# Attention scores made by two halves of TensorE's array instead of the whole one, in a gated cross-attention and mixture-of-experts layer

## What is computed

```python
qh = (q @ Wq + bq).reshape(B, LQ, 16, 32).transpose(0, 2, 1, 3)      # q = layernorm(x)
kh = (k @ Wk + bk).reshape(B, 128, 16, 32).transpose(0, 2, 1, 3)     # k = v = ctx_512
vh = (v @ Wv + bv).reshape(B, 128, 16, 32).transpose(0, 2, 1, 3)
attn = softmax(einsum('bhqd,bhkd->bhqk', qh, kh) / sqrt(32))
x = x + tanh(g_xattn[0]) * (concat(einsum('bhqk,bhkd->bhqd', attn, vh)) @ Wo + bo)
...
logits = clip(layernorm2(x) @ router_w.T); top_v, top_i = top_k(logits, 2)
# each expert takes its tokens in order, up to a capacity of 1280
h = silu(xb @ w_gate.T) * (xb @ w_up.T); yb = h @ w3.T
x = x + tanh(g_ffn[0]) * (sum of the two experts' rows, weighted)
```

## Time and profile before

| | us |
|---|---|
| median of 3 runs | 2701.61 (2700.34 to 2702.97) |
| the profiled execution | 2701.12 |
| its span, first to last instruction | 2698.4 |
| TensorE busy | 2606.9 (97% of the span) |
| VectorE busy | 1395.5 (52%) |
| ScalarE busy | 948.5 (35%) |
| GpSimd busy | 419.9 (16%) |

### The profile page before, as it was taken

One profiled execution on the slowest core, in us unless ns is written; L12 is line 12 of the kernel. 1 busy time (PEld: TensorE's weight loads), 2 busy tenths in 40 slices (PEclk: granted clock), 3 DMA queues, 4 the chain that ended last, 5 costly groups with the idle time before them and its releaser, 6 DMA issues.

```text
span 2698.4 us, 40582 instructions
## 1 busy us (share of the span) xinstructions
PE 2606.9 (97%) x14168; PEld 2319.0 (86%) x14169; DVE 1395.5 (52%) x2644; ACT 948.5 (35%) x2481; POOL 419.9 (16%) x399
## 2 busy tenths in 40 slices
PE   7999999499999999999999999999999999999988
PEld 6887887499999888888888888888888999989987
DVE  5898888444444444444444444443444444445555
ACT  6766666222224222242222322332223322233343
POOL 5555555300002000020000300010001100030030
PEclk9999999699999999999999999999999999999999
DMA  9422222411113210132101511231012311132142
GB/s 343 162 93 80 100 90 73 163 65 46 47 47 58 87 47 23 47 62 86 47 23 47 114 60 47 77 84 47 23 47 64 82 47 47 47 79 111 70 127 81
DMA packets 58993, 208.37 MB, mean 77 GB/s; under 512 B 8516, under 2 KB 8796, under 8 KB 50562
## 3 DMA queue, kind: packets, MB, share of 16 engines
q1 hardware_dynamic: 42242, 175.30, 18.1%
q0 software_dynamic: 16640, 31.69, 6.1%
HBM read 145.60 MB, written 67.70 MB: 79 GB/s over the span
## 4 chain that ended last, share of the span: by engine, by line
PE 77%; issue 2%; DVE 1%; ACT 1%; DMA 0%; DVEq 0%; ACTq 0%; POOL 0%; POOLq 0%
PE bank L1580 76%; PE bank L1586 1%; DVE yacc L1520 0%; ACT slotsT_hi L1412 0%; DVE slotsT_lo L1489 0%; DVE h L1540 0%; DMA xrow<-expert_rows 0%; ACT yout L1436 0%; ACT later_hi L1408 0%; ACT h_hi L1450 0%; POOL out_dram L1394 0%; DVE w_lo L1483 0%; ACT silu L1444 0%; DVE early_lo L1483 0%; ACTq L1292 0%
## 5 line engine op out<-in xcount | busy, mean ns | idle before, releaser
L1540 DVE TENSOR_TENSOR h<-silu,bank 128x384 f32<-128x384 f32 (+2 forms) x320 | 183.8, 575 | 829.3 <-PE bank L1580 819.5
L1580 PE MATMUL bank<-slotsT_hi,early_hi 128*128 128x384 f32 (+2 forms) x1280 | 445.1, 348 | 13.3 <-issue 11.5
L1580 PE MATMUL bank<-slotsT_hi,w_hi 128*128 128x384 f32 (+2 forms) x1280 | 442.6, 346 | 5.9 <-DVE w_lo L1483 5.9
L1580 PE MATMUL bank<-slotsT_lo,early_hi 128*128 128x384 f32 (+2 forms) x1280 | 443.2, 346 | 1.7 <-issue 1.7
L1580 PE MATMUL bank<-slotsT_hi,early_lo 128*128 128x384 f32 (+2 forms) x1280 | 442.4, 346 | 0.0
L1580 PE MATMUL bank<-slotsT_lo,w_hi 128*128 128x384 f32 (+2 forms) x1280 | 442.1, 345 | 0.0
L1580 PE MATMUL bank<-slotsT_hi,w_lo 128*128 128x384 f32 (+2 forms) x1280 | 441.2, 345 | 0.0
L1450 ACT CAST h_hi<-h 128x384 fp32r<-128x384 f32 (+2 forms) x320 | 169.3, 529 | 746.2 <-DVE h L1540 746.2
L1444 ACT ACTIVATE silu<-bank 128x384 f32<-128x384 f32 (+2 forms) x320 | 162.5, 508 | 729.2 <-PE bank L1580 728.7
L1394 POOL DMA_INDIRECT out_dram<-yout,token x63 | 97.9, 1554 | 1976.5 <-ACT yout L1436 1675.7
L1520 DVE TENSOR_TENSOR yacc<-bank,yacc 128x512 f32<-128x512 f32 x464 | 316.8, 689 | 168.8 <-PE bank L1580 168.7
(11 more groups left out here) (199 smaller groups left out, 3549.4 us busy)
## 6 DMA issues: line engine op xcount, KB each, us to landing
staged<-in_moe_w_dram SPq DMA_DIRECT2D x33, 1536.0 KB, 6.4
raw<-in_moe_w_dram SPq DMA_DIRECT2D x32, 1536.0 KB, 6.4
xrow<-expert_rows SPq DMA_DIRECT2D x42, 520.0 KB, 8.2
expert_rows<-zeros SPq DMA_DIRECT2D x40, 520.0 KB, 8.6
xin<-in_x_dram SPq DMA_DIRECT2D x17, 512.0 KB, 3.7
xres<-in_x_dram SPq DMA_DIRECT2D x15, 512.0 KB, 3.7
out_dram<-xres SPq DMA_DIRECT2D x15, 512.0 KB, 3.1
staged<-in_L_xattn_Wq_dram SPq DMA_DIRECT2D x1, 1024.0 KB, 7.3
```

Source lines behind the costliest of these rows:

```text
L1540: nc.vector.tensor_tensor(h32[q % 2][:, 0:W], silu[q % 2][:, 0:W], UB[q % 2][:, 0:W], ALU.mult)\
L1580: last = nc.tensor.matmul(out_ap, st, mv, start=(at == 0), stop=(at == n - 1))
```

## The change

TensorE's array is used as two halves of 64 rows. Rows 0 to 63 hold heads 0 and 1 of a group, rows 64 to 127 hold heads 2 and 3, and each half makes its two heads' scores with 256 moving columns, so that the zero blocks that lay between the two pairs of heads are no longer streamed. Half c writes PSUM bank c. One call `scores(n, g)` makes both token tiles of a group: 12 matmuls of 256 columns, the halves taking turns, in place of two calls of three matmuls of 512 columns. A bank now holds two heads of both tiles instead of four heads of one tile, and `maxima` and `exps` go by bank, with the same number of instructions and elements as before. The call waits until the exps of the whole group before are done. Both banks are signalled at the end of the stretch.

In VectorE's order three of the eight `maxima` of a block move up: the fourth, the sixth and the eighth stand right behind the one before them.

```diff
+            HP = HG // 2
...
                     def exps(blk, idx):
 
-                        g, t = divmod(idx, 2)
+                        g, c = divmod(idx, 2)
                         act.wait_ge(max_ready, 2 * KD * blk + idx + 1)
                         if not isinstance(blk, int) or blk > 0:
-                            act.wait_ge(pt_ready, 2 * KD * (blk - 1) + idx + 1)
-                        for hh in range(HG):
-                            h = HG * g + hh
-                            ins = nc.scalar.activation(probs[:, t, h, :], S_BANK[t][:, hh * LKV:(hh + 1) * LKV], ACT.Exp,
-                                                       bias=neg_max[:, t, h:h + 1], accum_out=sums[:, t, h:h + 1])
+                            act.wait_ge(pt_ready, 2 * KD * (blk - 1) + 2 * g + 2)
+                        for t in range(2):
+                            for hh in range(HP):
+                                h, at = HG * g + HP * c + hh, (HP * t + hh) * LKV
+                                ins = nc.scalar.activation(probs[:, t, h, :], S_BANK[c][:, at:at + LKV], ACT.Exp,
+                                                           bias=neg_max[:, t, h:h + 1], accum_out=sums[:, t, h:h + 1])
                         ins.then_inc(exp_done, 1)
...
                     def maxima(n, idx):
-                        g, t = divmod(idx, 2)
+                        g, c = divmod(idx, 2)
                         dve.wait_ge(s_ready, 2 * KD * n + idx + 1)
-                        nc.vector.tensor_reduce(neg_max[:, t, HG * g:HG * (g + 1)],
-                                                S_BANK[t][:, :].rearrange("p (h t) -> p h t", h=HG),
+                        nc.vector.tensor_reduce(neg_max[:, :, HG * g + HP * c:HG * g + HP * (c + 1)],
+                                                S_BANK[c][:, :].rearrange("p (t h k) -> p t h k", t=2, h=HP),
                                                 AX.X, ALU.max, negate=True).then_inc(max_ready, 1)
...
-                    def scores(n, idx, b):
-                        g, t = divmod(idx, 2)
+                    def scores(n, g, b):
 
                         pe.wait_ge(q_lo, KD * n + g + 1)
-                        if not isinstance(n, int) or 2 * KD * n + idx >= 2:
-                            pe.wait_ge(exp_done, 2 * KD * n + idx - 1)
-                        passes(S_BANK[t][:, :], [((qT_hi[:, g, t * P:(t + 1) * P], qT_lo[:, g, t * P:(t + 1) * P]),
-                                                  (k_hi[b][:, g, :], k_lo[b][:, g, :]))]).then_inc(s_ready, 1)
+                        if not isinstance(n, int) or KD * n + g >= 1:
+                            pe.wait_ge(exp_done, 2 * KD * n + 2 * g)
+                        for t in range(2):
+                            for i, (qs, ks) in enumerate(((qT_hi, k_hi), (qT_hi, k_lo), (qT_lo, k_hi))):
+                                for c in range(2):
+                                    rows, keys_of = slice(c * HP * DK, (c + 1) * HP * DK), slice(c * HP * LKV, (c + 1) * HP * LKV)
+                                    last = nc.tensor.matmul(S_BANK[c][:, t * HP * LKV:(t + 1) * HP * LKV],
+                                                            qs[rows, g, t * P:(t + 1) * P], ks[b][rows, g, keys_of],
+                                                            start=(i == 0), stop=(i == 2))
+                                    if t == 1 and i == 2:
+                                        last.then_inc(s_ready, 1)
```

More of the change, by code:

```diff
@@ L855, in step @@
                             maxima(n, 2)
+                            maxima(n, 3)
                             q_rest(n, 1)
@@ L860, in step @@
                             x_rest(n + 1)
-                        if has(n, 0):
-                            maxima(n, 3)
                         if isinstance(n, int) and n == 0:
@@ L871, in step @@
                             maxima(n, 4)
+                            maxima(n, 5)
                         if has(n, 2):
@@ L874, in step @@
                         if has(n, 0):
-                            maxima(n, 5)
                             recips(n, 1)
@@ L884, in step @@
                             maxima(n, 6)
+                            maxima(n, 7)
                         if has(n, 1):
@@ L889, in step @@
                             pT_second(n, 0)
-                            maxima(n, 7)
                         if has(n, -2):
@@ L1069, in step @@
                             scores(n, 0, b_s)
-                            scores(n, 1, b_s)
                             if has(n, -3):
@@ L1078, in step @@
                                 values_made(0)
-                            scores(n, 2, b_s)
+                            scores(n, 1, b_s)
                         if has(n, 1):
@@ L1089, in step @@
                             heads(n - 1, 0, b_v)
-                        if has(n, 0):
-                            scores(n, 3, b_s)
                         if has(n, -1):
@@ L1096, in step @@
                         if has(n, 0):
-                            scores(n, 4, b_s)
+                            scores(n, 2, b_s)
                         if has(n, -2):
@@ L1104, in step @@
                             turn_rows(n - 2)
-                        if has(n, 0):
-                            scores(n, 5, b_s)
                         if has(n, -1):
@@ L1117, in step @@
                             probs_T(n, 0)
-                            scores(n, 6, b_s)
+                            scores(n, 3, b_s)
                         if has(n, -1):
@@ L1122, in step @@
                             attention_out(n - 1, 0)
-                        if has(n, 0):
-                            scores(n, 7, b_s)
                         if has(n, -2):
```

## The result

| | before | changed |
|---|---|---|
| median of 4 runs | 2701.12 us (2700.34 to 2702.97) | 2729.01 us (2723.40 to 2731.17) |
| span of the profiled execution | 2698.4 | 2727.2 |
| mean granted TensorE clock | 0.983 | 0.980 |

The changed kernel is slower: the ratio is 1.0099, with a 95% interval of 1.0082 to 1.0117. The forecast was 2720 (2703 to 2738), +18 where +28 came.

A forecast was written before the change was run, and what follows sets the result against it. The prediction took a loop over VectorE and GpSimd, with TensorE closing it together, to bound the attention blocks. 13 blocks at 1.4 us more gave 18 us on 2701.1, hence 2720 us, range 2703 to 2738.

The forecast's parts named there:

- rival A: Attention blocks: VectorE's new order lengthens the loop over VectorE and GpSimd, 2710 to 2732 us; chance 0.60.
- Step 1: Score matmuls on TensorE: the two row halves run fully parallel, 0.72 us a group instead of 1.38.
- Step 2: Score stretches on TensorE: entering and leaving the 64-row array shape costs 0.40 us a stretch, or nothing.
- Step 3: Group 1's scores wait some 0.8 us for group 0's exps; maximum 2 comes 0.58 later, 0.31 remaining.
- Step 4: VectorE's order: maxima ahead of the statistics and `q_rest` cost 0.60 us each, not given back; `q_rest` 1.51 later.
- Step 5: TensorE's side of the loop: its saved time becomes idle time ahead of `attention_out`, which starts 1.51 us later.
- Sum: Blocks 2 to 14: 1.4 us more for each of 13 blocks, 18 us in all; nothing for other blocks.
- Rival B: Attention blocks: TensorE sets the time and gets faster, 2685 us, or 2659 without shape cost; chance 0.11.
- D: Score matmuls: the halves don't overlap, 1.84 us a group, 28 us more, 2748 us; chance 0.08.
- C: Delays absorbed: `place`'s count doesn't wait for GpSimd and three or four clock drops vanish, about 2703 us; chance 0.12.
- E: TensorE's clock drops in every block from longer idle time, 14 us more, 2734 us; chance 0.09.
- theory V: Experiments' theory: VectorE and GpSimd close the loop, two moved maxima cost 0.60 us each a block, late signals the rest.

The follow-up runs named there:

- experiment 9: Changed kernel with SyncE's store of a block's output rows issued some 5 us later, behind the load of rows: 2724.55 us, 1.0091 of the kernel before.
- experiment 5: Changed kernel without GpSimd's four indirect writes of routing rows a block: 2704.86 us, one run.
- experiment 2: Kernel before with only maximum 7 (the eighth) moved ahead of `q_rest` in VectorE's order: 2719.25 us, 1.0069 of the kernel before.
- experiment 3: Changed kernel with scores by full 128-row matmuls of 512 columns, tile by tile, instead of halves: 2714.85 us, 1.0048 of the kernel before.
- experiment 11: Kernel before with maximum 7 ahead of `q_rest` and the output store behind the load: 2721.28 us, 1.0073 of the kernel before.

## Why the prediction was right, and where it was off

**Direction and mechanism (rival A) held.** The loop over VectorE and GpSimd sets the block: VectorE's order undone gives back 1.2 us a block and 13.7 us in all, half of the 28. The size of the sum came out right in part by luck, as its bullet below says.

- *Step 1, halves parallel*: held. Pairs every 0.12 us.
- *Step 2, 0.40 for the change of shape*: close. The rows show 0.1 behind the first pair, 0.09 ahead of the query and 0.1 ahead of its follower, 1.0 us of TensorE with the pairs' 0.72. The fourth 0.1, ahead of the first pair, can't be told in them.
- *Step 3, stall ahead of group 1*: the stall is there (0.73 against 0.8). Maximum 2 was to come at 4.84 and comes at 4.76 where the signals are on time. In seven blocks it comes at 5.5, 0.7 later: 5 us. This is the term that was mis-sized in an undisturbed block, and what the signals do was in none of the rows of before.
- *Step 4, 0.60 twice, not given back*: held, to 0.01 us in the piece before `q_rest`.
- *Step 5, TensorE's saved time turns into idle time*: held; busy 26.20 of 30.11 us, and `attention_out` waits 1.40 us for `q_rest`.
- *Sum*: blocks 2 to 14 gave 21.9 where 18 were forecast. A block at clock 1.00 with signals on time takes 29.3 to 29.7, some 1.5 more than before, as the sum said. But the sum took over the clock's falls as they were, and 21.9 holds 5 us of late signals and about 7.5 us of five blocks at a fallen clock that took 1.3 to 1.6 more than their like, where five had taken 2.3 more each before. In the two runs with signals on time the same stretch took 9.7 and 17.1 us more than before. So the nearness of 21.9 to 18 is partly errors that cancel.
- *Outside the 13 blocks*: blocks 0 and 1, counted at nothing, cost 3.8, 3.2 of it in block 1, whose window has a granted clock of 0.85 instead of 0.97. In experiment 9, with the same scores and order, block 1 takes 27.1 us at 0.97 and not 30.0, so it goes with the clock and not with the work. The expert stage was taken as untouched; it took 2.8 longer.
- *Rival B* fell: TensorE's busy share dropped and the span rose. *D* fell with the pairs. *C* fell in its first half, since the count still waits for `norm`; its second, that time lost to the clock comes back, didn't show in the changed kernel (six of blocks 2 to 14 fell below 1.00, five before) but did in experiment 5, at 2705. *E* didn't come: seven of blocks 2 to 14 kept a clock of 1.00.

What stays open is, first, why the clock falls where it does: it is what theory V missed in experiments 2, 3 and 11, along with the late signals. The other is why the signals are late in nine of the fourteen profiles and in none of the other five. From block 4 on they are released 0.6 to 1.1 us after GpSimd's last indirect write ends (after 4.39, at 5.36 in the changed kernel's block 6, both counted from maximum 0; after 3.01, at 4.05 in experiment 2's block 6). TensorE's stall, the 64-row matmuls and the place of the store are ruled out as causes. A rival is untested: the nine traces also lack events. Of the landings of the indirect writes they have 502 to 588 of 1024, where the four other profiles with these writes have 1021 to 1024, and they lack 82 to 128 events of other semaphores, VectorE's and ScalarE's among them, where the others lack at most 4. Whether the signals are late in the chip alone or because their recording gets in the way, no run here tells.

## What to carry to other kernels

Ask of a change to the bound engine's work which instructions of other engines it makes move along. Here three maxima moved up, two of them, of 0.60 us each, ahead of work on a loop over VectorE and GpSimd. That cost 13.7 us, more than the 9 us of TensorE's busy time that the halves saved. Moving two maxima the other way was worth 0.35% (0.22 to 0.47) without touching TensorE. Where a short operation ends together with another engine's long one, it is held, and what stands between it and the loop's other end costs nothing.

## What the runs showed of the hardware

- Two 64-row halves of the array run fully beside each other: mostly 2 to 4 ns apart, a pair of 256 columns each every 0.12 us, like one full matmul (changed kernel).
- TensorE's semaphore signals can come up to 2.5 us behind the matmul's end while GpSimd issues indirect writes, with TensorE running on meanwhile. In the same kernels the trace also lacks about half of the landing events of these writes (563 of 1024 recorded in the changed kernel, 1021 in the kernel before). Whether a kernel has it changed with the place of one VectorE instruction (experiment 2).
- The same stretch of expert code stopped TensorE for 2.0 to 2.8 us or for 5.0 to 7.4, by what kernel stood ahead of it.
- A fall of TensorE's granted clock to a mean of 0.94 in a block cost 2.3 us in the kernel before (27.8 to 30.1) and nothing in a block of experiment 5 (29.30 at 0.94, 29.40 at 1.00).
